# Third stage of a four-layer graph kernel: projections of all heads before attention, and neighbour scores by transposed columns

## Chip, cores and metric

The kernel runs on one core of one Trainium2 chip, as one program with five engines: TensorE (matmuls and transposes into the eight banks of PSUM), VectorE, ScalarE, GpSimd (POOL in the rows) and SyncE, which starts the DMAs. The metric is the device time of one execution in microseconds, median of several runs.

## What is computed

`x` is 64 batches of 128 nodes with 256 values, `adj` one 128x128 adjacency matrix. Four layers follow each other, each as `x = x + layer(relu(layernorm(x)), adj)`. Layers three and four, which the change touches, are attentions whose score of node i for node j is a sum of one number of i and one of j:

```python
# layer 3 (H=4 heads, 256 values each), then the same once more with W_out, then a feed-forward part
Wh = einsum('bnf,hfo->bhno', x, W)
f1 = einsum('bhno,ho->bhn', Wh, a[:, :O]);  f2 = einsum('bhno,ho->bhn', Wh, a[:, O:])
e = f1[:, :, :, None] + f2[:, :, None, :]
e = where(e > 0, e, 0.01 * e);  e = where(adj[None, None] > 0, e, -1e9)
h = elu(einsum('bhnm,bhmo->bhno', softmax(e, axis=-1), Wh))
...
# layer 4: h = X @ W (128 values); e = leaky_relu(h@a0 + (h@a1)^T, 0.2), masked; softmax; concat([alpha @ h, h])
```

## The kernel before

Two batches are a group (`G = 2`), so each of the four stages runs over `NG = 32` groups; `x` stays in SBUF throughout. A stage is a pipeline written out by hand: `run_steps` calls a function `step2` (third stage) or `step3` (fourth stage) once a step on every engine, and in one step group g is at its first part, group g-1 at its second and so on. In `step2` the letters are `f` (group g: scores and softmax), `m` (g-1: heads), `o2` (g-2: product with `W_out`), `l` (g-3: second attention), `e` (g-4: feed-forward output). Every engine executes its queue in the order in which the code is written, and a semaphore wait stops all that stands behind it on that engine.

In the third stage a step of TensorE is, in this order: transposes of `h` (L1160); transposes of the softmaxed `probs` of group m (L1359); the `features`, the eight score numbers of a node, as fp32 matmuls with 32 weight columns (L1365); the feed-forward output of group e (L1374, L1376) with the aggregations of group m between, `agg` (L1323); the score matrix (mask L1386, sums L1389); two more aggregations; the second layer's scores (L1398, L1399); and then `out_product` (L1343) and `head` (L1330) in turn, with the second attention (L1413, L1424) and the first feed-forward product (L1436) at their places. `agg` multiplies the probabilities of all four heads with `h` (128x512 fp32), and `head(i)` then multiplies the aggregate by the head's weights.

The products by weights use a split: an operand is a high part of type fp32r plus a low part, and three single-pass matmuls (high x high, high x low, low x high) replace one fp32 matmul. ScalarE makes the high part by a cast (`high_agg` L980, `high_head` L993), VectorE the low part by a subtraction (`low_agg` L701, `low_head` L695). An fp32 matmul stands in the trace as two rows.

Scores need a number of each neighbour in a row, the same on all 128 partitions. Before, VectorE multiplies the identity by the column (`diag`, L813 in the third stage, L860 in the fourth), and TensorE multiplies a matrix of ones by that diagonal (L1399, L1455).

On ScalarE a step holds the copies out of PSUM, the exponentials (L1005 for the first attention, four with accumulated sums for each batch; `exp_head` L986 for the elu) and the activations that make the next `h` (L289). On VectorE it holds the leaky relu and maxima (L706, L708), normalisation (L714), the elu (`elu_head` L688, L690), and layer norm. GpSimd computes the small numbers of the layer norm and adds the results to `x` (L492, L495).

## Time and profile before

| | |
|---|---|
| median of 3 runs | 1662.28 us (1660.25 to 1665.63) |
| profiled execution | 1662.14 us, its span 1660.3 us |
| TensorE busy (matmul / weight load) | 1471.5 us (89%) / 1242.8 us (75%) |
| VectorE busy | 1283.4 us (77%) |
| ScalarE busy | 1021.6 us (62%) |
| POOL busy | 440.7 us (27%) |
| third stage, first and last feature product | 614.9 and 1416.3 us |
| fourth stage, score products | 1517.4 to 1650.4 us |

Busy times are unions of rows. The rows of matmuls overlap, since the next one starts long before the end of the one ahead is written, so the distance between two starts tells what one costs TensorE. "Idle before" names the engine and line whose result ended the idle time. `PEclk` is the granted clock of TensorE, 1 being 2.4 GHz.

### The profile page before, as it was taken

How to read it: one execution, taken by the hardware profiler on the slowest of the kernel's cores; microseconds unless marked ns; L12 is line 12 of the kernel's file. 1: busy time of each engine (PE TensorE's matmuls, PEld its weight loads, DVE VectorE, ACT ScalarE, POOL GpSimd, SP SyncE). 2: the span in 40 equal slices, each digit the busy share in tenths (PEclk: the TensorE clock that was granted, in tenths of full speed). 3: DMA queues.
4: the chain of work that ended last, by engine and by line, in shares of the span. 5: the costliest groups of instructions: out<-in, count | busy, mean ns of one | idle time of the engine just before them, and what ended most of it. 6: DMA issues, size and time to landing. Idle time of an engine off the chain costs nothing.

```text
span 1660.3 us, 36159 instructions
## 1 busy us (share of the span) xinstructions
PE 1471.5 (89%) x11454; PEld 1242.8 (75%) x11517; DVE 1283.4 (77%) x3002; ACT 1021.6 (62%) x3208; POOL 440.7 (27%) x745
## 2 busy tenths in 40 slices
PE   5789999999879977999999999999999999975776
PEld 4678888888779965787877777787877778764554
DVE  4877777777567758788888888888888888754997
ACT  3568788788645546565666556565666656533776
POOL 1112212212046642031222223132222222122332
PEclk9899999999979988999999999999999999996999
DMA  7400000000000000000000000000000000000112
GB/s 235 133 2 0 0 0 0 0 0 0 1 1 0 0 0 1 1 1 1 0 0 0 0 0 0 0 0 0 0 0 0 0 0 1 1 1 7 64 63 70
DMA packets 23873, 24.22 MB, mean 15 GB/s; under 512 B 1936, under 2 KB 23184, under 8 KB 23696
## 3 DMA queue, kind: packets, MB, share of 16 engines
q1 hardware_dynamic: 23824, 23.60, 4.5%
q8 instruction: 26, 0.43, 0.1%
q14 instruction: 23, 0.19, 0.0%
HBM read 15.21 MB, written 8.39 MB: 14 GB/s over the span
## 4 chain that ended last, share of the span: by engine, by line
PE 42%; DVE 26%; ACT 18%; issue 11%; POOL 1%; DVEq 0%; DMA 0%; ACTq 0%; SPq 0%; POOLq 0%
ACT probs L894 9%; PE bank L1323 4%; PE bank L1436 4%; PE bank L1160 3%; DVE headsT_lo L695 3%; PE bank L1374 3%; DVE probs L706 3%; PE bank L1246 2%; DVE em L688 2%; PE bank L1389 2%; PE bank L1237 2%; ACT probs L1005 2%; PE bank L1278 2%; PE bank L1290 2%; PE bank L1291 2%
## 5 line engine op out<-in xcount | busy, mean ns | idle before, releaser
L894 ACT ACTIVATE probs<-bank,negtop 128x128 f32<-128x128 f32 x512 | 185.8, 415 | 47.6 <-DVE negtop L628 47.5
L273 POOL TENSOR_TENSOR var_eps<-mv,eps_tile 128x2 f32<-128x2 f32 x128 | 38.3, 299 | 636.6 <-DVE mv L261 636.6
L1330 PE MATMUL bank<-aggT_hi,wh_hi 128*128 128x256 f32 x512 | 148.5, 290 | 12.2 <-DVE em L690 9.2
L289 ACT ACTIVATE h<-x_all,shift,rstd 128x256 f32 (+1 forms) x256 | 139.9, 596 | 31.5 <-POOL shift L279 31.5
L1343 PE MATMUL bank<-wout_hi,headsT_hi 128*128 128x258 f32 x512 | 156.2, 305 | 0.0
L980 ACT CAST aggT_hi<-bank 128x512 fp32r<-128x512 f32 x128 | 75.2, 588 | 120.3 <-PE bank L1323 120.3
L1330 PE MATMUL bank<-aggT_lo,wh_hi 128*128 128x256 f32 x512 | 145.1, 283 | 0.0
L1330 PE MATMUL bank<-aggT_hi,wh_lo 128*128 128x256 f32 x512 | 145.1, 283 | 0.0
L1343 PE MATMUL bank<-wout_lo,headsT_hi 128*128 128x258 f32 x512 | 144.5, 282 | 0.0
L1343 PE MATMUL bank<-wout_hi,headsT_lo 128*128 128x258 f32 x512 | 144.2, 282 | 0.0
L1323 PE MATMUL bank<-probsT,h 128*128 128x512 f32 x256 | 133.2, 625 | 0.5 <-ACT probsT L1013 0.5
L894 ACT ACTIVATION_READ_ACCUMULATOR probs<-bank,negtop 128x1 f32 x512 | 130.1, 254 | 0.0
L485 POOL TENSOR_TENSOR var_y<-mv_y,eps_tile 128x2 f32<-128x2 f32 x32 | 6.3, 196 | 466.3 <-DVE mv_y L755 466.3
L695 DVE TENSOR_TENSOR headsT_lo<-em,headsT_hi 128x512 fp32r<-128x512 f32 x128 | 127.6, 1014 | 2.7 <-ACT headsT_hi L993 2.4
L993 ACT CAST headsT_hi<-em 128x512 fp32r<-128x512 f32 x128 | 79.1, 618 | 61.8 <-DVE em L690 61.8
L1330 PEld LDWEIGHTS bank<-aggT_hi,wh_hi 128*128 128x128 f32 x512 | 97.4, 190 | 19.4 <-DVE em L690 15.6
L275 POOL TENSOR_TENSOR rstd<-var_eps,pow_half 128x2 f32<-128x2 f32 x128 | 104.6, 817 | 10.0
L701 DVE TENSOR_TENSOR aggT_lo<-bank,aggT_hi 128x512 fp32r<-128x512 f32 x128 | 86.6, 677 | 24.2 <-ACT aggT_hi L980 24.1
L1195 PE MATMUL bank<-consts,probs 128*128 128x128 f32 x512 | 75.7, 281 | 31.7 <-DVE probsT L584 17.1
L1160 PE MATMUL bank<-consts,h 128*128 128x128 f32 x384 | 64.6, 295 | 43.0 <-ACT h L289 43.0
L1005 ACT ACTIVATE probs<-probs,negtop 128x128 f32<-128x128 f32 x256 | 99.4, 400 | 1.0 <-DVE negtop L708 1.0
L1343 PEld LDWEIGHTS bank<-wout_lo,headsT_hi 128*128 128x128 f32 x512 | 97.3, 190 | 1.0 <-issue 0.2
(209 smaller groups left out, 4718.2 us busy)
## 6 DMA issues: line engine op xcount, KB each, us to landing
x_all<-in_x SPq DMA_DIRECT2D x32, 256.0 KB, 2.8
...
```

Source lines behind the costliest of these rows:

```text
L275: nc.gpsimd.tensor_tensor(rstd[:, p, :], var_eps[:, p, :], pow_half[:, :], ALU.pow).then_inc(s.norm, 1)
L289: last = nc.scalar.activation(h[:, p, c, :], x_all[:, bass.ds(g * G + c, 1), :].rearrange("p a d -> p (a d)"), ACT.Relu, bias=shift[:, p, ...
L695: nc.vector.tensor_tensor(headsT_lo[:, i].rearrange("p k c n -> p k (c n)"), em[:, i % 2], headsT_hi[:, i].rearrange("p k c n -> p k (c n) ...
L701: nc.vector.tensor_tensor(aggT_lo[:, dc, :, c, :], bank[3 + (2 + i) % 4][:, :].rearrange("p (h n) -> p h n", h=H2), aggT_hi[:, dc, :, c, : ...
L894: last = nc.scalar.activation(probs[:, r, i, :], bank[4 + r][:, i * N:(i + 1) * N], ACT.Exp, bias=negtop0[:, r, i:i + 1], scale=float(DH) ...
L993: nc.scalar.copy(headsT_hi[:, i].rearrange("p k c n -> p k (c n)"), em[:, i % 2]).then_inc(hd2_hi, 1)
L1005: last = nc.scalar.activation(probs[:, c, hh, :], probs[:, c, hh, :], ACT.Exp, bias=negtop2[:, c, hh:hh + 1], accum_out=sum2[:, c, hh:hh + 1])
L1160: last = nc.tensor.transpose(dst[:, (k * G + c) * N:(k * G + c + 1) * N], src[:, c, k * N:(k + 1) * N], ident)
L1195: last = nc.tensor.transpose(bank[2 + r % 2][:, k * N:(k + 1) * N], probs[:, r, k, :], ident)
L1323: nc.tensor.matmul(bank[3 + (2 + i) % 4][:, :], h[:, pm, c, dc * N:(dc + 1) * N], probsT[:, c].rearrange("p h n -> p (h n)"), start=True, ...
L1330: last = nc.tensor.matmul(bank[3 + i % 2][:, o * G * N:(o + 1) * G * N], w[:, k, i, o * N:(o + 1) * N], src[:, k, i].rearrange("p c n -> p ...
L1343: last = nc.tensor.matmul(bank[5 + c][:, 0:D + 2], src[:, i, o, c, :], w[:, k, :], start=(k == 0 and src is headsT_hi and w is wout_hi), s ...
```

## The change

In the third stage the order of the two products is turned round: `project(c)` multiplies `h` of a batch by the weights of all heads (24 matmuls with 512 moving columns a step) and ScalarE copies the result to `whs`, which is held twice; `head(i)` is then one fp32 matmul of 128 columns for each batch and half, with the probabilities as moving operand. `agg`, `high_agg` and `low_agg` are gone. The transposed `h` is now split into a high and a low part, and `features` uses this split with 64 weight columns instead of an fp32 copy `hT`. The low parts of the weights are made before the first group. In both the third and the fourth stage the diagonal is gone: `neighbours` transposes a column that is read 128 times (step 0) straight into the PSUM bank. The queues of TensorE, VectorE and ScalarE are put in a new order for this. The core of the diff:

```diff
-                if f:
-                    dve.wait_ge(hT2_full, g + 1)
-                    if positive(g):
-                        dve.wait_ge(f_full, g)
-                    nc.vector.tensor_copy(hT[:, :, :, :], bank[0][:, :].rearrange("p (k c n) -> p k c n", k=KC, c=G)).then_inc(hT2, 1)
...
+                if f:
+                    dve.wait_ge(hT2_high, g + 1)
+                    nc.vector.tensor_tensor(hT2_lo[:, :, :, :], bank[0][:, :].rearrange("p (k c n) -> p k c n", k=KC, c=G),
+                                            hT2_hi[:, :, :, :].bitcast(FP32), ALU.subtract).then_inc(hT2, 1)
...
-                    for c in range(G):
-                        last = nc.vector.tensor_scalar(diag[:, 0, c, :], ident, wh2[:, po, c, D + 1:D + 2], None, ALU.mult)
-                    last.then_inc(diag2, 1)
...
+                        dve.wait_ge(w_hi, i + 1)
+                        nc.vector.tensor_tensor(lo, w, hi.bitcast(FP32), ALU.subtract).then_inc(w_lo, 1)
...
-                if f:
-                    dve.wait_ge(h3_ready, g + 1)
-                    if positive(g - 1):
-                        dve.wait_ge(s4_full, g - 1)
-                    for c in range(G):
-                        last = nc.vector.tensor_scalar(diag[:, p, c, :], ident, h3[:, at.quarter(0), c, F3 + 1:F3 + 2], None, ALU.mult)
-                    last.then_inc(diag3, 1)
...
-                def high_agg(i):
-                    act.wait_ge(agg_full, gm * 4 + i + 1)
-                    if positive(gm) and i == 0:
-                        act.wait_ge(hd2_full, gm * 4)
-                    c, dc = i // 2, i % 2
-                    nc.scalar.copy(aggT_hi[:, dc, :, c, :], bank[3 + (2 + i) % 4][:, :].rearrange("p (h n) -> p h n", h=H2)).then_inc(agg_hi, 1)
+                def project_out(j):
+                    act.wait_ge(whs_full, g * 4 + j + 1)
+                    nc.scalar.copy(whs[:, p, j // 2, j % 2 * 2 * D:(j % 2 + 1) * 2 * D], bank[1 + j % 2][:, :]).then_inc(whs_ready, 1)
...
+                if f:
+                    act.wait_ge(hT2_full, g + 1)
+                    nc.scalar.copy(hT2_hi[:, :, :, :], bank[0][:, :].rearrange("p (k c n) -> p k c n", k=KC, c=G)).then_inc(hT2_high, 1)
...
-                if m:
-                    high_agg(3)
                 if l:
...
+                    scores_out(1)
                     exp_scores(0)
...
-                if f:
+                if m:
+                    high_head(0, gm)
+                    high_head(1, gm)
+                if f:
+                    project_out(0)
+                    project_out(1)
                     exp_scores(1)
...
+                n, gn, _ = at.group(-1)
+                if n and positive(gn - 1):
+                    act.wait_ge(hT2_full, gn - 1)
+                pre_act(act, 2, at)
...
+                if f:
+                    project_out(2)
+                    project_out(3)
...
+            def neighbours(dst, column, stop):
+                for c in range(G):
+                    last = nc.tensor.matmul(dst[:, c * N:(c + 1) * N], column[:, c, :].broadcast_to([N, N]), ident, is_transpose=True,
+                                            start=c == 0 or stop, stop=stop)
                 return last
...
-                def agg(i):
-                    c, dc = i // 2, i % 2
-                    if dc == 0:
-                        pe.wait_ge(pT2_ready, gm * 2 + c + 1)
-                    if i < 2 and positive(gm - 1):
-                        pe.wait_ge((wh2_act, wh2_dve)[i], gm - 1)
-                    nc.tensor.matmul(bank[3 + (2 + i) % 4][:, :], h[:, pm, c, dc * N:(dc + 1) * N],
-                                     probsT[:, c].rearrange("p h n -> p (h n)"), start=True, stop=True).then_inc(agg_full, 1)
+                def features():
+                    first = True
+                    for c in range(G):
+                        cols = slice((1 - c) * DH, (3 - c) * DH)
+                        for k in range(KC):
+                            for w, src in ((wf_hi, hT2_hi), (wf_lo, hT2_hi), (wf_hi, hT2_lo)):
+                                last = nc.tensor.matmul(bank[0][0:2 * DH, 0:N], w[:, k, cols], src[:, k, c, :], start=first,
+                                                        stop=(c == G - 1 and k == KC - 1 and src is hT2_lo))
+                                first = False
+                    last.then_inc(f_full, 1)
+
+                def project(c):
+                    for half in range(2):
+                        if c == 0:
+                            pe.wait_ge(scores2, g * 2 + 1 + half)
+                        else:
+                            pe.wait_ge(whs_ready, g * 4 + 1 + half)
+                        for k in range(KC):
+                            for src, w in ((hT2_hi, wh_hi), (hT2_hi, wh_lo), (hT2_lo, wh_hi)):
+                                last = nc.tensor.matmul(bank[1 + half][:, :], src[:, k, c, :],
+                                                        w[:, k, 2 * half:2 * half + 2, :].rearrange("p h o -> p (h o)"),
+                                                        start=(k == 0 and src is hT2_hi and w is wh_hi), stop=(k == KC - 1 and src is hT2_lo))
+                        last.then_inc(whs_full, 1)
 
                 def head(i):
+                    if i < 2:
+                        pe.wait_ge(pT2_ready, gm * 2 + 2)
+                        pe.wait_ge(whs_ready, gm * 4 + 4)
+                    else:
+                        pe.wait_ge(hd2_elu, gm * 8 + 2 * (i - 2) + 2)
                     for o in range(KC):
-                        for k in range(KC):
-                            for w, src in ((wh_hi, aggT_hi), (wh_lo, aggT_hi), (wh_hi, aggT_lo)):
-                                last = nc.tensor.matmul(bank[3 + i % 2][:, o * G * N:(o + 1) * G * N], w[:, k, i, o * N:(o + 1) * N],
-                                                        src[:, k, i].rearrange("p c n -> p (c n)"), start=(k == 0 and w is wh_hi and src is aggT_hi),
-                                                        stop=(k == KC - 1 and src is aggT_lo))
+                        for c in range(G):
+                            last = nc.tensor.matmul(bank[3 + i % 2][:, (o * G + c) * N:(o * G + c + 1) * N],
+                                                    whs[:, pm, c, i * D + o * N:i * D + (o + 1) * N], probsT[:, c, i, :],
+                                                    start=True, stop=True)
                     last.then_inc(hd2_full, 1)
...
-                            pe.wait_ge(agg_lo, gm * 4 + 1 + c)
+                        if i == 0 and positive(go):
+                            pe.wait_ge((wh2_act, wh2_dve)[c], go)
...
-                if f:
-                    pe.wait_ge(hT2, g + 1)
-                    for c in range(G):
-                        for k in range(KC):
-                            last = nc.tensor.matmul(bank[0][c * 32:(c + 1) * 32, 0:N], wh_f[:, k, :], hT[:, k, c, :],
-                                                    start=(k == 0), stop=(k == KC - 1))
-                    last.then_inc(f_full, 1)
-                if m:
-                    agg(0)
...
-                    agg(1)
+                if f:
+                    if not positive(g):
+                        pe.wait_ge(w_lo, 2)
+                    pe.wait_ge(hT2, g + 1)
+                    features()
+                if m:
+                    head(0)
+                    head(1)
                 if f:
                     pe.wait_ge(lr_step, g * 2 + 2)
                     if positive(g):
-                        pe.wait_ge(scores2, g * 2)
+                        pe.wait_ge(whs_ready, g * 4)
                     for c in range(G):
                         nc.tensor.matmul(bank[1 + c][:, :], ident_bf[:, :], hide2[:, :, :], start=True, stop=False)
                     for c in range(G):
                         rows = slice(c * 32, (c + 1) * 32)
                         nc.tensor.matmul(bank[1 + c][:, :], left[rows, :], right[rows].rearrange("p h n -> p (h n)"),
                                          start=False, stop=True).then_inc(s2_full, 1)
-                if m:
-                    agg(2)
-                    agg(3)
                 if l:
-                    pe.wait_ge(diag2, gl + 1)
+                    pe.wait_ge(wh2_act, gl + 1)
+                    pe.wait_ge(wh2_dve, gl + 1)
                     if positive(gl):
                         pe.wait_ge(y_step, gl * 3 - 2)
-                    nc.tensor.matmul(bank[7][:, 0:G * N], ident_bf[:, :], hide2[:, 0:G, :], start=True, stop=False)
-                    nc.tensor.matmul(bank[7][:, 0:G * N], ones[:, :], diag[:, 0].rearrange("p c n -> p (c n)"),
-                                     start=False, stop=True).then_inc(s3_full, 1)
+                    neighbours(bank[7], wh2[:, pl, :, D + 1:D + 2], stop=False)
+                    nc.tensor.matmul(bank[7][:, 0:G * N], ident_bf[:, :], hide2[:, 0:G, :], start=False, stop=True).then_inc(s3_full, 1)
                 if o2:
                     out_product(0)
                     out_product(1)
-                if m:
-                    if not positive(gm):
-                        pe.wait_ge(w_lo, 2)
-                    pe.wait_ge(agg_lo, gm * 4 + 4)
-                    head(0)
-                    head(1)
+                if f:
...
+                    head(2)
...
                 if m:
-                    pe.wait_ge(hd2_elu, gm * 8 + 2)
-                    head(2)
+                    head(3)
...
+                if f:
+                    project(1)
                 if o2:
                     out_product(3)
-                if m:
-                    pe.wait_ge(hd2_elu, gm * 8 + 4)
-                    head(3)
...
-                    pe.wait_ge(diag3, gm + 1)
+                    pe.wait_ge(h3_ready, gm + 1)
                     if positive(gm):
                         pe.wait_ge(scores4, gm)
-                    nc.tensor.matmul(bank[2][:, 0:G * N], ones[:, :], diag[:, pm].rearrange("p c n -> p (c n)"),
-                                     start=True, stop=True).then_inc(s4_full, 1)
```

On TensorE, from the feature product to the first output product of a step. Before:

```order
L1365 MATMUL bank<-hT,wh_f 32x128 [waits hT2]
...
L1323 MATMUL bank<-probsT,h 128x512 [waits wh2_act,pT2_ready]
L1374 MATMUL bank<-ffn,uT 128x256 [waits u_ready]
...
L1323 MATMUL bank<-probsT,h 128x512 [waits wh2_dve]
L1386 MATMUL bank<-hide,ident_bf 128x512 [waits scores2,lr_step]
...
L1389 MATMUL bank<-right,left 128x512 x2
L1323 MATMUL bank<-probsT,h 128x512 [waits pT2_ready]
...
L1398 MATMUL bank<-hide,ident_bf 128x256 [waits y_step,diag2]
L1399 MATMUL bank<-diag,ones 128x256
L1343 MATMUL bank<-wout_hi,headsT_hi 128x258 [waits agg_lo,hd2_lo]
```

After:

```order
L1372 MATMUL bank<-ffn,uT 128x256 [waits u_ready]
...
L1311 MATMUL bank<-hT_hi,wf_hi 64x128 [waits hT2]
L1311 MATMUL bank<-hT_hi,wf_lo 64x128
L1311 MATMUL bank<-hT_lo,wf_hi 64x128
...
L1337 MATMUL bank<-probsT,whs 128x128 [waits whs_ready,pT2_ready]
...
L1337 MATMUL bank<-probsT,whs 128x128 [waits whs_ready,pT2_ready]
...
L1390 MATMUL bank<-hide,ident_bf 128x512 [waits whs_ready,lr_step]
...
L1393 MATMUL bank<-right,left 128x512 x2
L1147 MATMUL bank<-consts,wh 128x128 [waits y_step,wh2_dve,wh2_act]
...
L1401 MATMUL bank<-hide,ident_bf 128x256
L1350 MATMUL bank<-wout_hi,headsT_hi 128x258 [waits wh2_act,hd2_lo]
```

The features (L1311 now, 12 matmuls) move behind the feed-forward output, heads 0 and 1 (L1337) take the place of the aggregations ahead of the scores, the diagonal's product becomes two transposes (L1147), and the output product no longer waits for `agg_lo`.

On TensorE, from the second attention's product to the first feed-forward product, whose wait for `outT` is called `at3_elu`. Before:

```order
L1424 MATMUL bank<-p3T,wh 128x128 [waits pT3_ready]
...
L1343 MATMUL bank<-wout_hi,headsT_hi 128x258 [waits hd2_lo]
...
L1330 MATMUL bank<-aggT_hi,wh_hi 128x256 [waits hd2_elu]
L1330 MATMUL bank<-aggT_hi,wh_lo 128x256
L1330 MATMUL bank<-aggT_lo,wh_hi 128x256
...
L1436 MATMUL bank<-outT,ffn 128x256 [waits at3_elu]
L1436 MATMUL bank<-outT,ffn 128x256 x3
```

After:

```order
L1422 MATMUL bank<-p3T,wh 128x128 [waits pT3_ready]
...
L1324 MATMUL bank<-wh_hi,hT_hi 128x512 [waits whs_ready]
L1324 MATMUL bank<-wh_lo,hT_hi 128x512
...
L1324 MATMUL bank<-wh_hi,hT_hi 128x512 [waits whs_ready]
...
L1350 MATMUL bank<-wout_hi,headsT_hi 128x258 [waits hd2_lo]
...
L1433 MATMUL bank<-outT,ffn 128x256 [waits at3_elu]
L1433 MATMUL bank<-outT,ffn 128x256 x3
```

The last head product is gone from here, and the second half of the projections (12 matmuls, L1324) stands in its place, ahead of the output product.

On ScalarE, from the exponentials of the first batch to the copy of `p3T`. Before:

```order
L1005 ACTIVATE probs,sum<-probs,negtop 128x128 [waits soft2]
L1005 ACTIVATE probs,sum<-probs,negtop 128x128 x3
L1048 ACTIVATE t,sum<-t,negtop 128x128 [waits top3]
...
L1005 ACTIVATE probs,sum<-probs,negtop 128x128 [waits soft2]
L1005 ACTIVATE probs,sum<-probs,negtop 128x128 x3
L986 ACTIVATE em<-bank 128x512 [waits hd2_lo,hd2_full] x2
L993 CAST headsT_hi<-em 128x512 [waits wo2_full,hd2_elu]
L1061 COPY p3T<-bank 128x256 [waits pT3_full]
L993 CAST headsT_hi<-em 128x512 [waits wo2_full,hd2_elu]
L986 ACTIVATE em<-bank 128x512 [waits hd2_lo,hd2_full]
L1069 ACTIVATE em<-bank 128x512 [waits at3_full]
```

After:

```order
L979 ACTIVATE probs<-bank 128x512 [waits s2_full]
L985 ACTIVATE probs,sum<-probs,negtop 128x128 [waits soft2]
L985 ACTIVATE probs,sum<-probs,negtop 128x128 x3
L1026 ACTIVATE t,sum<-t,negtop 128x128 [waits top3]
...
L973 CAST headsT_hi<-em 128x512 [waits wo2_full,hd2_elu] x2
L960 COPY whs<-bank 128x512 [waits whs_full] x2
L985 ACTIVATE probs,sum<-probs,negtop 128x128 [waits soft2]
L985 ACTIVATE probs,sum<-probs,negtop 128x128 x3
L966 ACTIVATE em<-bank 128x512 [waits hd2_lo,hd2_full]
L1042 COPY p3T<-bank 128x256 [waits pT3_full]
L291 ACTIVATE h<-x_all,shift,rstd 128x256 [waits norm2,hT2_full]
```

Two copies of projections (L960), which wait for TensorE, and the casts of heads 0 and 1 now stand ahead of the second exponentials, and the exponentials of heads 0 and 1 have moved up, ahead of the scores.

## Rows read from the trace of the kernel before

**Rows 1.** Windows: start:end, length, busy PE, PEld, DVE, ACT, POOL, clock, DMA.
```profile
1000.00:1200.00 200.00, 188.97 (x1268) 156.90 (x1274) 174.15 (x372) 124.33 (x350) 53.52 (x72) 1.00 0.00 0
```

**Rows 2.** TensorE in order of time, one step: start, length, line, operands, count.
```profile
1014.21 1.99 PE L1436 MATMUL bank<-outT,ffn 128*128 128x256 f32 x8 [1.05 <-DVE outT L801]
1016.04 0.60 PE L1160 MATMUL bank<-consts,h 128*128 128x128 f32 x4
1016.48 1.04 PE L1359 MATMUL bank<-consts,probs 128*128 128x128 f32 x8
1017.45 0.64 PE L1365 MATMUL bank<-hT,wh_f 128*32 128x128 f32 x8
1018.01 1.12 PE L1323 MATMUL bank<-probsT,h 128*128 128x512 f32 x2
1018.98 1.03 PE L1374 MATMUL bank<-ffn,uT 128*128 128x256 f32 x4
...
1024.04 1.98 PE L1323 MATMUL bank<-probsT,h 128*128 128x512 f32 x4
1025.86 0.27 PE L1398 MATMUL bank<-hide,ident_bf 128*128 128x256 bf16 x1
...
1026.21 0.47 PE L1343 MATMUL bank<-wout_hi,headsT_hi 128*128 128x258 f32 x1
...
1042.63 0.60 PE L1160 MATMUL bank<-consts,h 128*128 128x128 f32 x4
```

**Rows 3.** TensorE in order of time, before the third head product and after.
```profile
1007.11 0.28 PE L1343 MATMUL bank<-wout_hi,headsT_lo 128*128 128x258 f32 x1
1007.71 0.39 PE L1330 MATMUL bank<-aggT_hi,wh_hi 128*128 128x256 f32 x1 [0.33 <-DVE em L690]
...
1009.25 1.05 PE L1424 MATMUL bank<-p3T,wh 128*128 128x128 f32 x8
1010.06 0.36 PE L1343 MATMUL bank<-wout_hi,headsT_hi 128*128 128x258 f32 x1
```

**Rows 4.** Waits, 790 to 1400 us: total, times, longest.
```profile
PE bank L1436 <- DVE outT L801: 24.1, 23, 1.1
```

**Rows 5.** Groups of instructions, 1000 to 1100 us: busy us, mean ns, idle before.
```profile
L1005 ACT ACTIVATE probs<-probs,negtop 128x128 f32<-128x128 f32 x32 | 12.4, 399 | 0.0
...
L701 DVE TENSOR_TENSOR aggT_lo<-bank,aggT_hi 128x512 fp32r<-128x512 f32 x15 | 10.1, 676 | 2.2 <-ACT aggT_hi L980 2.2
...
L980 ACT CAST aggT_hi<-bank 128x512 fp32r<-128x512 f32 x14 | 8.2, 588 | 11.8 <-PE bank L1323 11.8
...
L813 DVE TENSOR_SCALAR diag<-consts,wh 128x128 f32<-128x128 f32 x8 | 1.9, 284 | 0.1
```

**Rows 6.** VectorE, then POOL, in order of time, while both work on SBUF.
```profile
1035.86 2.76 DVE L695 TENSOR_TENSOR headsT_lo<-em,headsT_hi 128x512 fp32r<-128x512 f32 x2
...
1034.96 1.40 POOL L492 TENSOR_TENSOR y<-y,gamma_row 128x512 f32<-128x512 f32 x1 [0.68 <-DVE y L787]
1036.55 1.52 POOL L495 TENSOR_TENSOR x_all<-x_all,y 128x512 f32 x1 [0.19 <-POOL y L492]
```

**Rows 7.** Fourth stage in order of time: VectorE, TensorE, ScalarE, and TensorE at its start.
```profile
1542.19 0.69 DVE L869 COPY hT<-bank 128x512 f32<-128x512 f32 x1 [0.31 <-PE bank L1160]
...
1546.32 0.69 DVE L869 COPY hT<-bank 128x512 f32<-128x512 f32 x1 [0.24 <-PE bank L1160]
...
1543.11 1.06 PE L1470 MATMUL bank<-w,hT 128*128 128x130 f32 x8
...
1545.63 0.66 PE L1160 MATMUL bank<-consts,h 128*128 128x128 f32 x4 [0.36 <-ACT h L289]
...
1544.48 1.09 ACT L289 ACTIVATE h<-x_all,shift,rstd 128x256 f32 x2
...
1516.68 1.11 PE L1160 MATMUL bank<-consts,h 128*128 128x128 f32 x4 [1.45 <-ACT h L289]
...
1522.13 1.11 PE L1160 MATMUL bank<-consts,h 128*128 128x128 f32 x4 [1.45 <-ACT h L289]
```

127 lines of the change are left out of this document (54 added, 73 removed).

## Prediction

> **What bounds the kernel now.** I read the windows of the trace first, to see how full each engine is while the third stage runs steadily, then TensorE's order of time through one step of it, then the waits, and last the costs of single operations. In a steady stretch of the third stage TensorE is busy 94% of the time at the full granted clock, VectorE 87%, ScalarE 62% [rows 1]. One step (one group of two batches enters, four older ones move on) lasts 26.59 us, from one block of transposes of `h` to the next [rows 2]. The matmul rows overlap, so I price by the distance from start to start, not by their own length. Priced so, TensorE has two idle places in a step: 1.05 us before the first feed-forward product, where it waits for `outT` from VectorE, 23 times in 23 steps, and 0.33 us before the third head product [rows 2 to 4]. Each also costs a restart: the second stretches the distance of starts from the usual 0.12 to 0.60 us (1007.11 to 1007.71), so it costs 0.48, 0.15 more than its row says, and the first by the same measure 1.20. All else, 24.9 us, is TensorE's own work. So TensorE bounds the stage, and VectorE, which feeds its largest wait, comes second. The stage has 28 steps in which all groups are there, and 8 at its ends.
>
> **Third stage, TensorE.** Removed from a step: the feature product (0.56 us, from 1017.45 to 1018.01); four aggregations of 128x512 fp32, two of them 1.82 us together and the first 0.97 us, so some 3.70 us; four head products of 12 matmuls, 1.46 us each without their restart, 5.84 us; the score row by the diagonal (0.35 us, 1025.86 to 1026.21); and both idle places, 1.68 us, if nothing takes their place [rows 2, 3]. That is 12.13 us.
>
> Added: 24 projections of 512 single-pass columns. No row has this form. The aggregation is fp32, each matmul of it stands as two rows, and one such row of 512 columns takes 1.82 / 4 = 0.455 us; a head matmul of 256 single-pass columns takes 1.46 / 12 = 0.12 us. Half the first is 0.2275, twice the second 0.24. I take 0.2275: 5.46 us (bounds 5.1 if the fixed part shrinks, 5.8 at 0.24). The head product becomes 4 fp32 matmuls of 128 columns, which is the form of the third stage's last attention product: 8 rows in 0.81 us [rows 3], so 3.24 us for four heads. The features become 12 single-pass matmuls of 128 columns and 64 weight columns, again without a row. Transposes of 128 columns with 128 weight columns take 0.11 us each (four in 0.44), and the present feature rows with 32 weight columns 0.07 [rows 2]; I take the side of the latter, 12 x 0.065 = 0.8 us, with bounds 0.7 and 2.7 (the second is a rival below). The score row becomes two transposes at 0.11 and the mask at 0.11: 0.33 us; reading one column 128 times is unseen here, and since a load of any other kind hides behind its neighbour I bound it at 0 and 0.3 us each. Sum of the added work: 9.83 us.
>
> The Trainium skill, page "TensorE: Matmul & The Clock Gate", section "Back-to-back issue gap", gives N / 2.4 + 2.5 ns for one matmul, by which the projections would cost 24 x 0.216 = 5.2 us, an estimate that would take 0.3 us more out of a step. Its next section has a load of P columns at P / 1.2 ns, so 64 weight columns would load in 53 ns and the features would be an estimated 0.7 us. The trace of before has neither form, so no row bears on them yet.
>
> **Third stage, the two engines that feed it.** VectorE loses four subtractions of 0.68 us and two diagonals of 0.28 us [rows 5], some 3.3 us of a step, and the copy of `hT` is replaced by a subtraction of the same size. ScalarE trades four casts of 0.59 us for four copies and gets one cast more. Both stay below TensorE in total. What matters is order, so I walked the new step with 0.6 us for a 128x512 operation on either engine and 1.55 us for a batch's four exponentials (0.40 each) [rows 5], time zero at the transposes of `h`. Features end on TensorE at 4.8; VectorE's three operations after them end at 6.5, while heads 0 and 1 cover TensorE until 6.4: wait about 0.1. ScalarE runs densely from 10.6 (first exponentials) through the casts of heads 0 and 1, two copies of projections, the second exponentials, head 2 and the copy of `p3T`, which ends at 17.4; TensorE gets there at 17.3: wait about 0.1. VectorE delivers `outT` at 21.8; TensorE arrives at 22.3, since the second projection and the last output product now stand between. So the 1.05 us wait should be gone, with 0.5 us to spare.
>
> That spare is thin. Two subtractions that both read SBUF (`headsT_lo`) take 2.76 us together while POOL adds `y` to `x`, where such a one takes 0.68 alone [rows 5, 6]: 1.4 us too much. POOL's two operations on `y` now start after VectorE's normalisation of `y` at 18.9 and last 3.0 us, so they fall on the second normalisation of the probabilities and on what leads to `outT`. I take 0.3 us of wait there, 0.5 us of new waits in all (bounds 0 and 1.4). The step: 26.59 - 12.13 + 9.83 + 0.5 = 24.79 us, 1.80 us less. Over 28 steps: 50.4 us. The 8 steps at the ends wait on chains, not on TensorE; there the features wait for the split weights (later by a few us), the first steps do no aggregation (earlier by as much). I take them at +1 us, bounds -4 and +5.
>
> **Fourth stage.** A step lasts 4.13 us, from one copy of `hT` to the next [rows 7], and is closed by a loop: the copy of `hT` on VectorE (0.69), the product with `w3` (start 1543.11), ScalarE's copy and its two activations of the next `h` (from 1544.48, 1.09), the transposes (1545.63), the copy again (1546.32). The diagonal is not in this loop. Taking its two operations (0.28 each) off VectorE brings the exponentials, and the transposes of the probabilities that stand before the product with `w3`, some 0.4 us forward; the product starts 0.23 us after the copy ends, where a handover takes 0.05. So 0.18 us a step can go, 32 x 0.18 = 5.8 us (bounds 0 and 10); the rest of the diagonal is hidden.
>
> Profiled execution 1662.1 us (span 1660.3), as good as the median of 1662.28: 1662.1 - 50.4 - 5.8 + 1 = 1606.9, so 1607 us.
>
> **Rivals.**
> *More waits than I walked.* If the in-order ScalarE queue, where projection copies stand ahead of the second exponentials, is later by 0.9 us a step, 25 us come back: 1632. For it: my slack is 0.1 to 0.5 us at three places. Against: I used handovers seen in the trace.
> *Features at four passes.* If a single-pass matmul below 256 columns is no faster than fp32, its 128 columns cost what 512 do, 12 x 0.2275 = 2.73 us, 1.93 more. The step is then 26.7 us, all of the gain of the stage gone: 28 x 0.13 = +4, fourth stage -6, ends +1: 1661. For it: every single-pass matmul of the trace has 256 or more columns and all narrower ones are fp32 or transposes. Against: no row shows such a penalty.
> *POOL slows VectorE in front of `outT`* (the slower side). If all 2.9 us of VectorE's work from 18.9 to 21.8 runs at the rate of the disturbed pair (2.76 for 1.28, a factor 2.2), `outT` comes at 25.2 and TensorE waits 2.9 us instead of 0.5: a step of 27.2 us, 28 x 0.6 = +17, with the rest 1674. It decides from 2.3 us of delay. Against: in the same stretch of POOL's work operations with one PSUM operand keep their length, and most of these 2.9 us are such.
> *The clock in the fourth stage.* Its granted clock stays full now. At its start, under the half clock, two transposes of `h` lie 5.45 us apart [rows 7] instead of 4.13. If the swap of a matmul for two transposes lets it fall, 32 x 1.5 = 48 us are lost: 1655. The Trainium skill, same page, "Part 4: PE-mode transpose", says that transposes don't count as busy for the clock; the fourth stage already has them in each step and keeps the clock, so I give this little.
>
> **How the numbers follow.** My forecast 52%, more waits 20%, slow features 18%, POOL 7%, clock 3%. The forecast's own range is 1588 to 1622 by the bounds above. The range for 8 in 10 takes in the waits, the clock and most of the feature case: 1586 to 1662. A measurement tells about 0.3%, 5 us, from no change. Faster: 52 + 20 + 3 and a third of the feature case, 80%; same half of that case and a little more, 10%; slower the POOL case and the rest, 10%.
>
> **What would show it.** Right: a step of 24.6 to 25.1 us, projections 0.22 to 0.23 us apart, feature matmuls 0.06 to 0.08 apart, at most 0.3 us of wait before the feed-forward product, a fourth-stage step near 3.95. Wrong: features 0.2 us apart; a wait for `p3T`, `right` or `outT` of over half a microsecond; broadcast columns that load slower than other weights; a granted clock below 1 in the middle of a stage.

## The result, and the profile after

The changed kernel takes 1638.5 us (median of 4 runs, 1635.6 to 1640.1), beside 1664.0 for the kernel before; the ratio is 0.985, with a 95% interval of 0.982 to 0.987. It is faster by 25 us, where 55 were forecast: the direction was right, the size was not half reached. The profiled execution has a span of 1635.7 us, 24.6 less than before.

First the same window as in [rows 1], of the kernel after.

```profile
1000.00:1200.00 200.00, 188.61 (x1304) 166.23 (x1311) 159.82 (x325) 123.34 (x341) 53.60 (x65) 1.00 0.00 0
```

TensorE is as full as before (94%), VectorE has 14 us less to do in 200, the clock is full. So the bound looks the same. TensorE in order of time shows what a step is made of now; it answers to [rows 2, 3].

```profile
1007.60 0.60 PE L1141 MATMUL bank<-consts,h 128*128 128x128 f32 x4
...
1011.45 0.30 PE L1311 MATMUL bank<-hT_hi,wf_hi 128*64 128x128 f32 x1
1011.59 0.22 PE L1311 MATMUL bank<-hT_hi,wf_lo 128*64 128x128 f32 x1
1011.65 0.22 PE L1311 MATMUL bank<-hT_lo,wf_hi 128*64 128x128 f32 x1
...
1012.25 2.00 PE L1337 MATMUL bank<-probsT,whs 128*128 128x128 f32 x16
1014.35 0.38 PE L1390 MATMUL bank<-hide,ident_bf 128*128 128x512 bf16 x1
...
1015.71 0.43 PE L1147 MATMUL bank<-consts,wh 128*128 128x128 f32 x2
...
1018.96 0.39 PE L1324 MATMUL bank<-wh_hi,hT_hi 128*128 128x512 f32 x1
1019.20 0.39 PE L1324 MATMUL bank<-wh_lo,hT_hi 128*128 128x512 f32 x1
...
1021.75 1.05 PE L1337 MATMUL bank<-probsT,whs 128*128 128x128 f32 x8
1022.64 0.38 PE L1412 MATMUL bank<-consts,t 128*128 128x128 f32 x2
...
1031.79 1.99 PE L1433 MATMUL bank<-outT,ffn 128*128 128x256 f32 x8 [1.33 <-DVE outT L797]
1033.62 0.60 PE L1141 MATMUL bank<-consts,h 128*128 128x128 f32 x4
```

The step lasts 26.02 us (1007.60 to 1033.62), 0.57 less than before; forecast were 1.80 less. The new products cost what was forecast (below). But the wait ahead of the feed-forward product, which was to shrink from 1.05 to 0.3 us, has grown to 1.33, in every step, as TensorE's waits from 790 to 1400 us say (total, times, longest; compare [rows 4]):

```profile
PE bank L1433 <- DVE outT L797: 31.7, 24, 1.3
```

So the question is why VectorE delivers `outT` late. Its own order of time up to `outT`, in the same step:

```profile
1025.26 0.69 DVE L692 TENSOR_TENSOR em<-bank,em 128x512 f32<-128x512 f32 x1
1025.87 0.73 DVE L784 TENSOR_SCALAR y<-y,mv_y,rstd_y 128x256 f32<-128x256 f32 x2
1026.51 0.17 DVE L708 RECIPROCAL rsum<-sum 128x4 f32<-128x4 f32 x1
1026.72 1.80 DVE L710 TENSOR_TENSOR probs<-probs,rsum 128x512 f32<-128x512 f32 x1
1028.44 1.51 DVE L690 TENSOR_SCALAR em<-em 128x512 f32<-128x512 f32 x1
1029.98 0.69 DVE L692 TENSOR_TENSOR em<-bank,em 128x512 f32<-128x512 f32 x1
1030.59 0.41 DVE L793 TENSOR_SCALAR em<-em 128x512 f32<-128x512 f32 x1
1031.04 0.69 DVE L797 TENSOR_TENSOR outT<-bank,em 128x512 f32<-128x512 f32 x1
```

And GpSimd beside it:

```profile
1026.68 1.29 POOL L494 TENSOR_TENSOR y<-y,gamma_row 128x512 f32<-128x512 f32 x1 [1.40 <-DVE y L784]
1028.16 1.50 POOL L497 TENSOR_TENSOR x_all<-x_all,y 128x512 f32 x1 [0.19 <-POOL y L494]
```

VectorE never idles here, so no wait names a culprit. What stands out are two lengths. The normalisation of the probabilities (L710) takes 1.80 us where the other one of the same step (1022.02) takes 0.69, and the tensor_scalar on `em` (L690) takes 1.51 where the others take 0.43. Each began just after a GpSimd operation, and each ended a little after that operation: GpSimd ends at 1027.97, and L710 0.55 later; GpSimd ends at 1029.66, and L690 0.29 later. It looks like an operation that is held until GpSimd's is through, and [rows 6] can be read the same way: GpSimd ended there at 1036.36 and 1038.07, the pair at 1038.62.

Not all that VectorE does in SBUF beside GpSimd gets longer. Earlier in the same step a reduction that reads SBUF alone lies wholly beside a GpSimd operation of the same size:

```profile
1019.55 1.42 POOL L304 TENSOR_TENSOR x_all<-x_all,beta_row 128x512 f32 x1
1019.84 0.69 DVE L704 TENSOR_REDUCE negtop<-probs 128x4 f32<-128x512 f32 x1
```

It takes 0.69 us, as the other reduction of the step does (1017.60), where nothing is beside it. Nor is L702 held, a scalar_tensor_tensor with two operands in SBUF: it starts at 1019.12 beside a GpSimd operation on two columns (L489, 0.70 us from 1018.88), and takes its 0.68 us.

My theory (H in the texts below): VectorE is held to the end of the GpSimd operation, the two holds are 1.10 + 1.09 us (1.80 less the 0.70 and 1.51 less the 0.42 that the two take unheld in e2 below), and they are what came instead of the gain. The rivals: the wait has another origin, ScalarE's chain or VectorE's queue (R); the hold only moves (M); GpSimd slows all that VectorE does beside it (S).

### The profile page after: what moved, and what is told of

Its sections match the earlier page's. It is cut to its first block, busy times and chain, and to the rows that moved or that the text cites. A ratio compares the mean times of both kernels' runs of the same rounds, so it can differ in the third digit from the quotient of the medians.

```text
span 1635.7 us, 36230 instructions
## 1 busy us (share of the span) xinstructions
PE 1449.0 (89%) x11581; PEld 1276.4 (78%) x11645; DVE 1202.6 (74%) x2747; ACT 1024.2 (63%) x3241; POOL 454.5 (28%) x747
## 4 chain that ended last, share of the span: by engine, by line
PE 43%; DVE 26%; ACT 17%; issue 12%; DVEq 1%; POOL 1%; DMA 0%; ACTq 0%; SPq 0%; POOLq 0%
ACT probs L877 9%; PE bank L1433 4%; DVE em L690 4%; PE bank L1337 4%; PE bank L1372 4%; PE bank L1141 3%; DVE probs L702 2%; PE bank L1234 2%; PE bank L1225 2%; DVE st L248 2%; PE bank L1393 2%; PE bank L1266 2%; PE bank L1279 2%; PE bank L1278 2%; PE bank L1280 2%
## 5 line engine op out<-in xcount | busy, mean ns | idle before, releaser
L966 ACT ACTIVATE em<-bank 128x512 f32<-128x512 f32 x128 | 75.7, 591 | 98.9 <-PE bank L1337 98.5
L1337 PE MATMUL bank<-probsT,whs 128*128 128x128 f32 x1024 | 132.8, 278 | 0.0
L1337 PEld LDWEIGHTS bank<-probsT,whs 128*128 128x128 f32 x1024 | 125.9, 194 | 2.7
L690 DVE TENSOR_SCALAR em<-em 128x512 f32<-128x512 f32 x128 | 85.2, 666 | 33.4 <-ACT em L966 29.9
L1324 PE MATMUL bank<-wh_hi,hT_hi 128*128 128x512 f32 x256 | 104.7, 409 | 1.4 <-ACT probs L979 1.4
L1324 PE MATMUL bank<-wh_hi,hT_lo 128*128 128x512 f32 x256 | 101.8, 398 | 0.0
L1433 PE MATMUL bank<-outT,ffn 128*128 128x256 f32 x256 | 65.5, 400 | 40.8 <-DVE outT L797 40.8
L1324 PE MATMUL bank<-wh_lo,hT_hi 128*128 128x512 f32 x256 | 101.6, 397 | 0.0
L1350 PEld LDWEIGHTS bank<-wout_hi,headsT_hi 128*128 128x128 f32 x512 | 96.8, 189 | 2.4 <-issue 0.8
L627 DVE TENSOR_REDUCE negtop<-bank 128x4 f32<-128x512 f32 x128 | 88.4, 690 | 12.1 <-PE bank L1234 12.1
```

Source lines behind the costliest of these rows:

```text
L627: nc.vector.tensor_reduce(negtop0[:, r, :], bank[4 + r][:, :].rearrange("p (k n) -> p k n", k=4), AX.X, ALU.max, negate=True).then_inc(top ...
L690: nc.vector.tensor_scalar(em[:, i % 2], em[:, i % 2], 1.0, -1.0, ALU.min, ALU.add).then_inc(hd2_elu, 1)
L966: nc.scalar.activation(em[:, i % 2], bank[3 + i % 2][:, :].rearrange("p (k n) -> p k n", k=KC), ACT.Exp).then_inc(hd2_exp, 1)
L1324: last = nc.tensor.matmul(bank[1 + half][:, :], src[:, k, c, :], w[:, k, 2 * half:2 * half + 2, :].rearrange("p h o -> p (h o)"), start=(k ...
L1337: last = nc.tensor.matmul(bank[3 + i % 2][:, (o * G + c) * N:(o * G + c + 1) * N], whs[:, pm, c, i * D + o * N:i * D + (o + 1) * N], probs ...
L1350: last = nc.tensor.matmul(bank[5 + c][:, 0:D + 2], src[:, i, o, c, :], w[:, k, :], start=(k == 0 and src is headsT_hi and w is wout_hi), s ...
```

## The experiments

Each ratio is against the kernel before in the same series of runs (medians 1659.5 to 1661.9 us; 1664.0 for the changed kernel's own). A step is read from one block of transposes of `h` to the next, or from one feed-forward product to the next.

| kernel | third-stage step, us | TensorE's waits in it | time, us | ratio (95%) |
|---|---|---|---|---|
| before | 26.59 | 1.05 `outT`, 0.33 `em` | 1659.5 to 1661.9 | 1 |
| after | 26.02 | 1.33 `outT` | 1638.5 | 0.985 (0.982 to 0.987) |
| e1 after, `y` late | 24.43 | none | 1592.2 | 0.960 (0.958 to 0.961) |
| e2 after, GpSimd's `y` work small | 24.43 | none | 1590.8 | 0.958 (0.957 to 0.960) |
| e3 before, `y` late | 26.02 | 0.69 `hT`, 0.31 `em` | 1643.6 | 0.991 (0.989 to 0.992) |
| e4 before, neighbours only | 26.57 | 1.05 `outT`, 0.52 `em` | 1657.7 | 0.998 (0.997 to 1.000) |
| e5 after, two operations swapped | 24.43 | none | 1592.7 | 0.959 (0.956 to 0.961) |
| e6 after, GpSimd in pieces | 24.43 | none | 1592.7 | 0.958 (0.956 to 0.960) |
| e7 e1 without the neighbours' part | 24.60 | none | 1598.1 | 0.961 (0.959 to 0.963) |
| e8 before, GpSimd's `y` work small | 25.37 | 0.31 `em` | 1622.8 | 0.977 (0.975 to 0.980) |
| e9 before, GpSimd in pieces | 25.66 | 0.32 `em` | 1635.8 | 0.985 (0.982 to 0.987) |

**e1: the operation that starts GpSimd, moved behind `outT`.** The edit, in VectorE's queue of the third stage:

```diff
-                if e:
-                    dve.wait_ge(y_norm, ge * 2 + 2)
-                    for c in range(G):
-                        last = nc.vector.tensor_scalar(y[:, c, :], y[:, c, :], mv_y[:, c, 0:1], rstd_y[:, c:c + 1],
-                                                       ALU.subtract, ALU.mult)
-                    last.then_inc(yn_ready, 1)
                 if f:
                     normalise(1)
...
                     low_head(2, gm)
+                if e:
+                    dve.wait_ge(y_norm, ge * 2 + 2)
...
+                    last.then_inc(yn_ready, 1)
```

> The changed kernel with VectorE's normalisation of y (the two tensor_scalar behind which GpSimd's two operations on y start) moved from ahead of normalise(1) to behind low_head(2); all is computed. Theory H (VectorE's operations that read two SBUF operands, or a tensor_scalar from SBUF to SBUF, are held until the GpSimd operation beside them ends): the third-stage normalise(1) falls from 1.80 to about 0.7 us and the em tensor_scalar from 1.51 to about 0.4, TensorE's wait for outT falls from 1.33 to 0 to 0.2, the step from 26.02 to 24.5 to 24.9, the time from 1638 to 1597 to 1607. Theory R (the wait is set by the ACT chain or by what is queued ahead on VectorE, whatever GpSimd does): the wait stays at 1.2 to 1.4 and the time within 4 us of 1638. Theory M (the hold moves with GpSimd's operations and meets the low heads or the output copies): the outT wait goes but another of 0.5 to 1.3 takes its place, 1612 to 1635.

It took 1592.2 us, below H's 1597 to 1607. VectorE's order of time in this kernel:

```profile
1027.74 0.69 DVE L710 TENSOR_TENSOR probs<-probs,rsum 128x512 f32<-128x512 f32 x1
1028.35 0.42 DVE L690 TENSOR_SCALAR em<-em 128x512 f32<-128x512 f32 x1
...
1029.87 0.69 DVE L791 TENSOR_TENSOR outT<-bank,em 128x512 f32<-128x512 f32 x1
...
1031.08 0.73 DVE L798 TENSOR_SCALAR y<-y,mv_y,rstd_y 128x256 f32<-128x256 f32 x2
```

Both operations are back at 0.69 and 0.42 us, and TensorE's window is full to the brim:

```profile
1000.00:1200.00 200.00, 200.00 (x1405) 177.75 (x1404) 153.88 (x354) 135.44 (x383) 58.03 (x76) 1.00 0.00 0
```

R and M fall: the wait was not ScalarE's, and nothing took its place. This kernel computes all, and is 46 us faster than the changed one. By itself the move could have helped in another way than by GpSimd, since it also takes the 0.65 us of that operation out of the way to `outT`. The next run shuts that out.

**e2: the order kept, GpSimd's two operations made small.** Most of the product of `y` with gamma and of its sum with `x` is left out.

```diff
-                        nc.gpsimd.tensor_tensor(y[:, :], y[:, :], gamma_row[:, :, :].broadcast_to([N, G, D]),
-                                                ALU.mult).then_inc(yg_ready, 1)
+                        nc.gpsimd.tensor_tensor(y[:, :, 0:2], y[:, :, 0:2], gamma_row[:, :, 0:2].broadcast_to([N, G, 2]),
+                                                ALU.mult).then_inc(yg_ready, 1)
...
```

> The changed kernel with GpSimd's two operations on y (times gamma, added to x) shrunk from 256 to 2 of the columns of a row, so most of that product and sum is left out; the order of all engines stays. Theory H (VectorE held to the end of the GpSimd operation): normalise(1) and the em tensor_scalar back to about 0.7 and 0.4 us in the third stage, the wait for outT to 0 to 0.2, the step to 24.5 to 24.9; the other stages lose their share of such holds too, time 1590 to 1607. Theory R (the ACT chain): the wait for outT stays at 1.2 to 1.4, step 26.0, time 1630 to 1638.

It took 1590.8 us. VectorE, in the order of the changed kernel:

```profile
1032.04 0.73 DVE L784 TENSOR_SCALAR y<-y,mv_y,rstd_y 128x256 f32<-128x256 f32 x2
...
1032.89 0.70 DVE L710 TENSOR_TENSOR probs<-probs,rsum 128x512 f32<-128x512 f32 x1
1033.52 0.42 DVE L690 TENSOR_SCALAR em<-em 128x512 f32<-128x512 f32 x1
...
1035.03 0.69 DVE L797 TENSOR_TENSOR outT<-bank,em 128x512 f32<-128x512 f32 x1
```

From the normalisation of `y` to `outT` are 2.99 us here (1032.04 to 1035.03) and 5.17 in the changed kernel (1025.87 to 1031.04). The difference, 2.18, is the sum of the two holds (1.10 + 1.09). TensorE starts the feed-forward product 0.75 us after `outT` is there (1035.72; the product starts at 1036.47). So of the 2.19 us of hold 0.75 is covered and some 1.4 are not: the wait's row says 1.33, and the step differs by 1.59. From start to start the two places differ by as much: in the changed kernel the feed-forward product starts 1.61 us after the last output product (1030.18 to 1031.79), where matmuls of that kind follow each other by 0.12, and then takes 1.83 us to the next start instead of 1.73.

**e5: one operation swapped.** The normalisation of `y` goes behind that of the probabilities, one place later; nothing else.

```diff
-                if e:
-                    dve.wait_ge(y_norm, ge * 2 + 2)
...
-                    last.then_inc(yn_ready, 1)
                 if f:
                     normalise(1)
+                if e:
+                    dve.wait_ge(y_norm, ge * 2 + 2)
...
+                    last.then_inc(yn_ready, 1)
                 if m:
                     elu_head(3)
```

> The changed kernel with the normalisation of y one place later than it stood, behind the third-stage normalise(1), so that GpSimd's two operations on y start about 0.7 us later and meet the last em tensor_scalar (SBUF to SBUF) and the two operations that read a bank of PSUM (em sum, outT). All is computed. Theory H, that VectorE is held only where all that it reads lies in SBUF: normalise(1) back to 0.69, the two operations with a PSUM operand at their 0.69 beside GpSimd, the em tensor_scalar at 0.42 if it starts before GpSimd does and at up to 1.7 if after; so the wait for outT falls to 0 to 0.3 in the first case (time 1592 to 1605) and stays near 0.7 in the second (about 1615). Theory S, that GpSimd slows whatever VectorE does beside it: the em sum and outT take over 1.2 us each and the wait for outT stays at 1 or more, time 1630 to 1640.

It took 1592.7 us. The order of time of VectorE and GpSimd shows which operations are held and which are not:

```profile
1031.33 0.42 DVE L690 TENSOR_SCALAR em<-em 128x512 f32<-128x512 f32 x1
1031.49 1.41 POOL L494 TENSOR_TENSOR y<-y,gamma_row 128x512 f32<-128x512 f32 x1 [2.21 <-DVE y L786]
1031.78 0.69 DVE L692 TENSOR_TENSOR em<-bank,em 128x512 f32<-128x512 f32 x1
1032.39 0.80 DVE L793 TENSOR_SCALAR em<-em 128x512 f32<-128x512 f32 x1
1033.09 1.30 POOL L497 TENSOR_TENSOR x_all<-x_all,y 128x512 f32 x1 [0.19 <-POOL y L494]
1033.22 0.69 DVE L797 TENSOR_TENSOR outT<-bank,em 128x512 f32<-128x512 f32 x1
1033.83 1.10 DVE L697 TENSOR_TENSOR headsT_lo<-em,headsT_hi 128x512 fp32r<-128x512 f32 x1
```

L692 and L797, which read a bank of PSUM, lie wholly beside a GpSimd operation and keep their 0.69 us. L690 began first and keeps its 0.42. L793, all in SBUF, began while GpSimd worked and takes 0.80: GpSimd ends at 1032.90, it ends 0.29 later. L697, with two operands in SBUF, takes 1.10: GpSimd ends at 1034.39, it ends 0.54 later. So S falls: GpSimd doesn't slow all that VectorE does beside it, but an operation of these two kinds is held until the other engine's is over. One hold of 0.38 us is still ahead of `outT`, and fits into the spare 0.75.

**e6: the same work of GpSimd in pieces.** Each of its two operations becomes four of 128 columns.

```diff
...
-                        nc.gpsimd.tensor_tensor(x_group(g), x_group(g), y[:, :], ALU.add).then_inc(pre[2].x, 1)
+                        for c in range(G):
+                            for d in range(0, D, D // 2):
+                                last = nc.gpsimd.tensor_tensor(x_group(g)[:, c, d:d + D // 2], x_group(g)[:, c, d:d + D // 2],
+                                                               y[:, c, d:d + D // 2], ALU.add)
+                        last.then_inc(pre[2].x, 1)
```

> The changed kernel with GpSimd's two operations on y cut into four pieces of 128 columns each; all is computed, in the same order. Theory H (held to the end of the GpSimd instruction, free between two): normalise(1) waits for one or two pieces of about 0.4 us, not for 1.3, and ends about 0.6 to 0.9 us earlier, the wait for outT falls from 1.33 to 0.2 to 0.8, time 1600 to 1625. Theory S (the two share a rate, so that VectorE's work takes longer by as much as GpSimd moves beside it): the same columns are moved, normalise(1) and the em tensor_scalar stay at 1.5 to 1.8 us, the wait at 1.2 or more, time 1635 or more.

It took 1592.7 us, better than H's 1600 to 1625. GpSimd, then VectorE (lines are 7 higher here):

```profile
1029.78 2.35 POOL L496 TENSOR_TENSOR y<-y,gamma_row 128x128 f32<-128x128 f32 x4 [1.39 <-DVE y L791]
...
1029.83 0.97 DVE L717 TENSOR_TENSOR probs<-probs,rsum 128x512 f32<-128x512 f32 x1
1030.72 0.68 DVE L697 TENSOR_SCALAR em<-em 128x512 f32<-128x512 f32 x1
```

GpSimd is beside VectorE for longer than before (2.35 us for 1.29), and VectorE loses less: 0.28 and 0.26 us instead of 1.10 and 1.09. A shared rate would have it the other way round. GpSimd pays: its pieces take 0.45 to 0.91 us, the long ones where VectorE got in between. So the hold works in both directions. In the changed kernel it stands too: the sum with `x` takes 1.50 us beside the held operations, and 1.27 in e1, where nothing is held.

**e8 and e9: what the hold cost the kernel before.** The edits of e2 and of e6, made on the kernel before (e8 leaves out most of the product and the sum as e2 does).

> The kernel before with GpSimd's two operations on y shrunk to 2 of the 256 columns (most of that product and sum left out), order unchanged: what the hold cost the kernel before. Theory H: the pair of low heads back from 2.76 to 1.36 us, the wait for outT from 1.05 to 0 to 0.1, step 26.59 to 25.3 to 25.6, time 1624 to 1636. Together with the same edit on the changed kernel (1590.8) it gives the change without the hold: 1590.8 to 1630 is 39 to 45 us by this theory; 55 to 57 would be the forecast's own figure.

> The kernel before with GpSimd's two operations on y cut into four pieces of 128 columns each, as in the sixth experiment; all is computed. Theory H (VectorE held to the end of one GpSimd instruction): the first low head of the pair waits for a piece of about 0.5 us instead of for an operation of 1.4, the pair takes 1.6 to 2.0 us for 2.76, the wait for outT falls from 1.05 to 0 to 0.4 and the time to 1623 to 1638; against the sixth experiment's 1592.7 that leaves 30 to 45 us for the change between two kernels of which neither is held. If the kernel before isn't helped (1655 or more), the 39 us of the experiment with 2 columns came from the lighter work of GpSimd and not from the end of the hold.

e8 took 1622.8 us, its step 25.37: the hold cost the kernel before 1.22 us a step, 28 x 1.22 = 34 us, and 39 us in all with what stands outside the full steps. The pair of low heads is two separate operations again, in VectorE's order of time:

```profile
1045.53 0.69 DVE L690 TENSOR_TENSOR em<-bank,em 128x512 f32<-128x512 f32 x1
1046.13 0.68 DVE L695 TENSOR_TENSOR headsT_lo<-em,headsT_hi 128x512 fp32r<-128x512 f32 x1
1046.98 0.69 DVE L695 TENSOR_TENSOR headsT_lo<-em,headsT_hi 128x512 fp32r<-128x512 f32 x1 [0.16 <-ACT headsT_hi L993]
```

e9 took 1635.8, within what was expected; one tensor_scalar is still held there by 0.26 us, which is what its step has over that of e8 (0.29). Without the hold on either side the change is worth 1622.8 - 1590.8 = 32 us, with GpSimd in pieces on both 1635.8 - 1592.7 = 43, as it was made 25. The 32 is a miss of the text of e8, which had 39 to 45: the kernel before gained more by the end of its hold than was expected (1624 to 1636). It also says that the forecast's 55 us wasn't all the change's own to give, hold or no hold.

**e3: the move of e1 on the kernel before.**

> The kernel before with the same move alone: VectorE's normalisation of y behind low_head(2). All is computed. Theory H: the wait for outT of 1.05 us falls to 0 to 0.2, the step from 26.59 to 25.2 to 25.6, 28 steps take 28 to 39 us off, time 1625 to 1636; so the changed kernel gained over before only what the longer hold left of it. Theory R: within 4 us of 1664. Theory M (other VectorE work is held in its place, the pair of low heads or the output copies): 1640 to 1664.

It took 1643.6 us: 16 us off, less than H's 28 to 39. It is M's number, but mostly not by M's mechanism. The wait for `outT` is gone and another has come, TensorE in order of time:

```profile
1033.08 1.89 PE L1436 MATMUL bank<-outT,ffn 128*128 128x256 f32 x8
1034.80 0.60 PE L1160 MATMUL bank<-consts,h 128*128 128x128 f32 x4
1036.96 0.64 PE L1365 MATMUL bank<-hT,wh_f 128*32 128x128 f32 x8 [0.69 <-DVE hT L721]
```

The feature product of the kernel before follows the transposes of `h` closely, and VectorE, which has the late `y` to do first (0.65 us), copies `hT` too late for it. The copy itself is not held: it takes 0.68 us (1036.22). The hold has moved too, to an operation with two SBUF operands behind it, which takes 1.15 us instead of 0.68 and for which TensorE shows no wait:

```profile
1038.51 1.15 DVE L730 TENSOR_TENSOR right<-right_rows,consts 64x512 f32<-64x512 f32 x1
```

The feature product starts 1.41 us after the transposes of `h` in the kernel before [rows 2], in the changed kernel 3.85 us (1007.60 to 1011.45), so the same move costs it nothing.

**e4 and e7: the parts apart.** e4 is the kernel before with only the neighbour scores changed, e7 is e1 with only the projections, the diagonals as before.

```diff
-                    nc.tensor.matmul(bank[7][:, 0:G * N], ident_bf[:, :], hide2[:, 0:G, :], start=True, stop=False)
-                    nc.tensor.matmul(bank[7][:, 0:G * N], ones[:, :], diag[:, 0].rearrange("p c n -> p (c n)"),
-                                     start=False, stop=True).then_inc(s3_full, 1)
+                    neighbours(bank[7], wh2[:, pl, :, D + 1:D + 2], stop=False)
+                    nc.tensor.matmul(bank[7][:, 0:G * N], ident_bf[:, :], hide2[:, 0:G, :], start=False, stop=True).then_inc(s3_full, 1)
...
```

> The kernel before with only the second part of the change: the neighbour scores by a transpose of the column read 128 times, in the third and the fourth stage, without VectorE's diagonal blocks; the third stage keeps its old product. All is computed. If the parts add up, it gives the fourth stage's 5.4 us (step 4.06 for 4.13 us) and in the third stage 0.05 a step or less from TensorE's shorter s3 (0.35 to 0.30), together 5 to 8 us: 1656 to 1659. If VectorE's freed 0.56 us a step of diagonal work in the third stage lets outT come earlier, up to 28 x 0.56 = 16 us more: 1641 to 1650.

> The first experiment's kernel (changed kernel, y normalisation behind low_head(2)) with the neighbour scores made as before, by VectorE's diagonal blocks and a product with ones, in both stages: so the projections-first part alone, without the hold. All is computed. If the parts add up: fourth-stage step 4.13 for 4.06 us (plus 2 to 3 us, with the entry 5), third-stage step longer by TensorE's 0.05 us and, if VectorE's 0.56 us for the diagonals stands ahead of what TensorE waits for, up to 0.3 more: 1598 to 1610 against 1592.

e4 took 1657.7 us for 1659.5 (ratio 0.997 to 1.000): hardly to be told from no change, less than the 5 to 8 us expected. Its profiled span is 4.9 us shorter. In the third stage it gains nothing, and its waits say why (from 790 to 1400 us):

```profile
PE bank L1430 <- DVE outT L801: 24.0, 23, 1.1
PE bank L1324 <- DVE em L690: 12.0, 23, 0.5
```

The wait for `outT` stays, that for `em` grows from 0.33 to 0.52: what is taken off TensorE and VectorE comes back as wait. The pair of low heads is held there as before (2.76 us at 1035.29). That it sets the step is what e8 suggests; e4 without the hold wasn't run. e7 took 1598.1 us, 5.9 over e1, as expected. With TensorE full, the neighbours' part is worth 0.17 us a step in the third stage (24.60 to 24.43), 4.8 us. The score row itself accounts for 0.07 of it (0.37 us from 1022.23 to 1022.60 in e7, 0.30 from 1017.39 to 1017.69 in e1). The rest is the output product behind it: its first matmul is followed by the next after 0.31 us in e7 (1022.60 to 1022.91) and in the kernel before, and after 0.20 in e1 (1017.69 to 1017.89). The prediction priced the row alone and counted 0.02 us for the swap.

## Why the prediction was right and wrong

**TensorE's own work: right in its sum.** The projections start 0.23 us apart (1019.20, 1019.43; 0.2275 taken); the 12 feature matmuls last 0.80 us from 1011.45 to 1012.25 (0.80 taken); the mask and the two broadcast transposes take some 0.3 us (0.33 taken). Two terms were short. The projections with a restart each come to 5.65 us (2.79 and 2.86 in e1, 5.46 taken), and the head products to 3.65 us in e1, 1.87 for two and 0.89 for each of the others (1021.75 to 1022.64 in the kernel after), where 3.24 was taken. What stayed of the old step made it good: 26.59 - 12.13 = 14.46 us were left by the sum, and 24.43 - 5.65 - 3.65 - 0.80 - 0.30 = 14.03 by e1; 0.11 of these 0.43 are the output product behind the score row. Without the wait for `outT` the forecast had a step of 24.79 - 0.30 = 24.49 us, and the runs without the hold show 24.43. That they agree to 0.06 us is in part luck: the terms that were short (0.60 together) are offset by these 0.43 and by 0.2 us of other waits that didn't come. The two estimates that the prediction set beside its sum, 0.216 us a projection and 0.7 us for the features, were both a little short.

**The wait for `outT`: the step that failed.** The sentence was "I take 0.3 us of wait there, 0.5 us of new waits in all (bounds 0 and 1.4)". The term measured 1.59 us (26.02 to 24.43), of which 1.33 stand in the row and the rest is the restart (0.26; the prediction's measure for one was 0.15). The step came out 26.02 - 24.79 = 1.23 us longer than forecast. 28 x 1.23 = 34 us is more than the whole miss of 31; the ends of the stage gave some of it back (below). The prediction had seen the place, the operations and even the pair of [rows 6]; it went wrong in what it made of them. It took the 1.4 us too much of that pair as a price for the whole encounter and as a rate (factor 2.2) for a rival, and it argued that most of the work ahead of `outT` reads PSUM and is safe. Most is, but the operation that starts GpSimd now had two operations right behind it that read SBUF alone, one for each GpSimd operation. Read as a hold, with ends and not with factors, the rows give it: the first operation waits out 1.3 us of GpSimd, the second 1.1 to 1.3 more, 2.2 to 2.4 us together, against the 0.5 us to spare that the walk found. 1.7 us of wait would have been the term, and 1607 + 28 x 1.4 = 1646 the time, an estimate made with the result known. It measured 1638.5. The walk itself was sound: it found 0.5 us to spare, and e2 shows 0.75.

The Trainium skill has the rule, on the page "SBUF — State Buffer", section "SBUF: two separate sides": the port pair that VectorE and GpSimd share is an exclusive lock, and of a GpSimd instruction and a VectorE instruction that has two SBUF inputs or runs in a two-port mode, whichever starts first has it for the whole instruction. The trace agrees with it: held operations end 0.29 to 0.55 us after GpSimd's, operations that read PSUM keep their 0.69 us beside it, and so does a reduction with one SBUF operand; GpSimd's pieces are held in turn. That the tensor_scalar runs in such a mode is shown here only by its being held. For L702 beside L489 a hold would follow from the rule, and the trace shows none.

**What was taken for a gain was a hold as well.** The 1.05 us of wait in the kernel before was counted as removed, because the second projection now stands ahead of the product that waited. What made it wasn't asked. e8, where the pair takes 0.68 and 0.69 us and the wait is gone, shows that it was the held pair of low heads. So the new order removed it and paid it again, in the same place and by the same mechanism.

**Rivals.** *POOL slows VectorE* (7%) had the right engines and the right place, but as mechanism a rate and not a hold: by a factor over 2.9 us it came out slower than before, 1674, where two holds took a part of the gain. *More waits than I walked* (1632, 20%) had the size, for a wrong reason: ScalarE's queue, where e2 shows no wait once the hold is gone. *Features at four passes* is refuted by matmuls 0.06 us apart; *the clock* by a granted clock of 1.00 in the third stage, as in the window above, and by one of 1.00 from 1550 to 1600 us, in the fourth stage.

**The ends of the stage** gave 3.2 us (19.2 for the whole stage, by the first transposes of the fourth, less 28 x 0.57 = 16.0), where +1 was taken with a bound of -4. It lies where the pipeline drains: from feed-forward product to feed-forward product the first short step takes 19.75 us instead of 22.92. **The fourth stage** gave 5.4 us, 5.8 taken, and is the second term that was mis-sized: the total agrees by luck. VectorE's copies of `hT` in the kernel after, the two of one step, then the last of the stretch:

```profile
1537.27 0.69 DVE L852 COPY hT<-bank 128x512 f32<-128x512 f32 x1 [0.42 <-PE bank L1141]
1541.33 0.69 DVE L852 COPY hT<-bank 128x512 f32<-128x512 f32 x1 [0.42 <-PE bank L1141]
...
1574.23 0.69 DVE L852 COPY hT<-bank 128x512 f32<-128x512 f32 x1 [0.42 <-PE bank L1141]
```

In the kernel before, the ends of a stretch of as many steps:

```profile
1537.97 0.69 DVE L869 COPY hT<-bank 128x512 f32<-128x512 f32 x1 [0.23 <-PE bank L1160]
...
1575.76 0.69 DVE L869 COPY hT<-bank 128x512 f32<-128x512 f32 x1 [0.15 <-PE bank L1160]
```

The steps of this stage are not alike: they take 4.06 us or 4.2 to 4.5 before, and 4.06 or 4.29 after, so one pair of copies, as in [rows 7], is no measure. Over the nine steps of each stretch they take 4.20 us before and 4.11 after, 0.09 us less where 0.18 was taken: 32 x 0.09 = 2.9 us. Another 2.0 us come from the first five steps of the stage, 25.59 us before and 23.59 after, and they belong to the clock and not to the change. The granted clock of the kernel before is 0.50 from 1512 to 1529 us and 1.00 from 1534; in e8, which runs the same fourth stage, it is at 1.00 for the third step (1485.7 to 1489.8), and its first five take 22.62 us; in e3, with the same fourth stage too, they take 22.98. So some 3 of the 5.4 us are the change's.

**What stays open.** Why the output product's first matmul is followed faster behind the transposed columns than behind the diagonal's product isn't shown. Nor is why L702 isn't held: whether it is its own kind or the two columns of GpSimd's operation that makes the difference wasn't tried. e6 and e9 leave a few holds of 0.3 us, which weren't taken out one by one.
